# Attention and feed-forward layer on eight cores: score and value matmuls issued in groups of two key tiles

## The reference

```python
x = x + attn(layernorm(x), Wq, Wk, Wv, Wo)     # 16 heads of 64, rotary, softmax over 4096 keys
x = x + ffn(layernorm(x), w1, b1, w2, b2)      # two bitlinear layers, GELU between them
# bitlinear: activations rounded to 8 bits by row, weights to -1, 0, 1 times a scale
h = bitlinear(x, w1, b1)                       # 1024 -> 4096
h = gelu(h, approximate=False)
return bitlinear(h, w2, b2)                    # 4096 -> 1024
```

## Time and profile before

| | |
|---|---|
| median of the timed runs | 2846.5 us (2844.7 to 2848.4) |
| the profiled execution | 2838.8 us |
| its span on the slowest core, core 2 | 2837.2 us |
| spans of the 8 cores | 2820.6 to 2837.2 us |
| mean granted TensorE clock, core 2 | 0.853 |

### The profile page before, as it was taken

The page is one execution under the profiler, slowest core; times in us unless marked ns, Lnnn a source line. Parts: engine busy times, 40 slices in busy tenths (PEclk is TensorE's granted clock), DMA queues, the critical chain, the costliest instruction groups (busy, mean ns, idle before and its releaser), DMA issues.

```text
span 2837.2 us, 33149 instructions; the slowest of 8 cores (2820.6 to 2837.2 us)
## 1 busy us (share of the span) xinstructions
PE 2228.4 (79%) x8940; PEld 759.5 (27%) x8940; DVE 1067.8 (38%) x1941; ACT 1599.9 (56%) x2139; POOL 180.3 (6%) x345
## 2 busy tenths in 40 slices
PE   4679999888888888888888888563047988889888
PEld 1223333222222222222222222121013433334333
DVE  2434445311111111102222220287536666666564
ACT  3301112489988899988899889311413444434432
POOL 4211111000000000000000000111100000000000
PEclk8799999889988889888899889776557888888888
DMA  9633323301001010101111110475600000000000
GB/s 160 94 60 60 60 60 73 99 23 45 30 30 52 23 45 30 53 1 56 41 60 45 45 31 1 112 231 184 200 37 1 31 31 16 31 18 28 31 16 23
DMA packets 72194, 160.57 MB, mean 57 GB/s; under 512 B 8144, under 2 KB 41040, under 8 KB 70736
## 3 DMA queue, kind: packets, MB, share of 16 engines
q0 software_dynamic: 48544, 104.90, 16.2%
q1 hardware_dynamic: 23472, 53.55, 5.2%
HBM read 158.42 MB, written 29.36 MB: 66 GB/s over the span
## 4 chain that ended last, share of the span: by engine, by line
PE 42%; ACT 28%; DVE 12%; issue 10%; DMA 6%; DVEq 1%; ACTq 1%; POOL 0%; POOLq 0%; SPq 0%
ACT Et L686 24%; PE ps_b L1271 9%; PE ps_b L1318 8%; PE ps_k L405 6%; PE ps_v L380 4%; PE ps_tr L1302 3%; PE ps_cA L621 2%; PE ps_S L656 2%; DMA xb<-x_fm 2%; PE ps_cB L627 2%; DMA w2st<-w2T 2%; DVE wtmp L878 1%; DVE q1fm L1154 1%; PE ps_k L412 1%; PE ps_n L421 1%
## 5 line engine op out<-in xcount | busy, mean ns | idle before, releaser
L686 ACT ACTIVATE Et<-ps_S,negG 128x1024 bf16<-128x1024 f32 x1024 | 1046.7, 1174 | 85.8 <-PE ps_S L661 78.9
L656 PE MATMUL ps_S<-Qp,Kp 64*128 64x512 bf16 x1024 | 411.8, 407 | 120.4 <-ACT Et L686 72.3
L621 PE MATMUL ps_cA<-Et,V_sb 128*65 128x512 bf16 x1024 | 436.0, 426 | 43.6 <-DVEq L768 37.0
L661 PE MATMUL ps_S<-Qp,Kp 64*128 64x512 bf16 x1024 | 423.1, 418 | 0.0
L627 PE MATMUL ps_cB<-Et,V_sb 128*65 128x512 bf16 x1024 | 413.8, 404 | 0.0
L756 DVE COPY rlbc<-ps_rl 64x512 f32<-64x512 f32 x32 | 21.8, 683 | 766.3 <-PE ps_rl L638 766.3
L1271 PE MATMUL ps_b<-w1q,q1fm 128*128 128x512 bf16 x1024 | 255.3, 415 | 1.2 <-DVEq L1156 1.0
L656 PEld LDWEIGHTS ps_S<-Qp,Kp 64*128 64x128 bf16 x1024 | 93.6, 94 | 595.0 <-issue 595.0
L493 ACT ACTIVATE ksq<-krot 128x512 bf16<-128x512 bf16 x96 | 60.4, 629 | 297.1 <-DVEq L461 297.1
L1318 PE MATMUL ps_b<-w2q,q2fm 128*128 128x512 bf16 x1024 | 226.2, 382 | 2.0 <-DVEq L1186 2.0
L621 PEld LDWEIGHTS ps_cA<-Et,V_sb 128*65 128x65 bf16 x1024 | 113.3, 111 | 302.0 <-issue 295.4
(11 more groups left out here) (193 smaller groups left out, 2155.3 us busy)
## 6 DMA issues: line engine op xcount, KB each, us to landing
w1st_<-w1T POOLq DMA_DIRECT2D x64, 512.0 KB, 4.2
w2st<-w2T POOLq DMA_DIRECT2D x64, 512.0 KB, 4.7
xb<-x_fm POOLq DMA_DIRECT2D x64, 128.0 KB, 9.8
xr<-x_fm POOLq DMA_DIRECT2D x64, 128.0 KB, 5.5
kscr<-krot SPq DMA_DIRECT2D x64, 128.0 KB, 1.9
Kp<-kscr SPq DMA_DIRECT2D x8, 1024.0 KB, 4.9
xq<-x_tmq SPq DMA_DIRECT2D x16, 512.0 KB, 6.7
y1scr<-y1r SPq DMA_DIRECT2D x16, 512.0 KB, 5.9
```

Source lines behind the costliest of these rows:

```text
L621: e.matmul(ps2_cA[:], V_sb[:, jj * VBLK + (2 * m) * VW: jj * VBLK + (2 * m) * VW + VW], Et[itp % 4][:, 0:512], start=(jj == 0), stop=(jj = ...
L656: e.matmul(ps2_S[it % 2][:, 0:512], Kp[m % 2][0:64, j * 128:(j + 1) * 128], Qp[m % 2][0:64, qh * 512:(qh + 1) * 512], start=True, stop=Tru ...
L661: e.matmul(ps2_S[it % 2][:, 512:1024], Kp[m % 2][64:128, j * 128:(j + 1) * 128], Qp[m % 2][64:128, qh * 512:(qh + 1) * 512], start=True, s ...
L686: e.activation(Et[it % 4][:], ps2_S[it % 2][:], AF.Exp, bias=negG[:, m:m + 1], scale=1.0).then_inc(SM["aEX"], 1)
```

## The change

It has two parts. In the attention stage TensorE's loop goes over pairs of key tiles. For jp = 0, 2, ... 30 it issues AV(jp-4), AV(jp-3), S(jp), S(jp+1), so the order is S0, S1, rl_a; S2, S3, rl_b; AV0, AV1, S4, S5; AV2, AV3, S6, S7; and so on; after S31 come AV28 to AV31. The buffers, the waits in front of each instruction and the other engines' programs stay as they are. In the last stage the bias rows are spread through the two tiles of `ps4_b1` in place of `ps4_b2`, and the wait for the last round moves from the second product of tile 0 to its first.

```diff
-                    for j in range(NTT):
-                        it = it_of(m, qh, j)
-                        ...
-                        e.matmul(ps2_S[it % 2][:, 0:512], ...)
-                        e.matmul(ps2_S[it % 2][:, 512:1024], ...).then_inc(SM["pSC"], 1)
-                        if j >= 3:
-                            do_av(j - 3)
-                        if blk >= 1 and j == 1:
+                    for jp in range(0, NTT, 2):
+                        for jj in (jp - 4, jp - 3):
+                            if jj >= 0:
+                                do_av(jj)
+                        for j in (jp, jp + 1):
+                            it = it_of(m, qh, j)
+                            ...
+                            if it >= 2:
+                                e.wait_ge(SM["aEX"], it)
+                            e.matmul(ps2_S[it % 2][:, 0:512], ...)
+                            e.matmul(ps2_S[it % 2][:, 512:1024], ...).then_inc(SM["pSC"], 1)
+                        if blk >= 1 and jp == 0:
                             rl_mm_a(blk - 1)
-                        if blk >= 1 and j == 2:
+                        if blk >= 1 and jp == 2:
                             rl_mm_b(blk - 1)
-                    for jj in (NTT - 3, NTT - 2, NTT - 1):
+                    for jj in (NTT - 4, NTT - 3, NTT - 2, NTT - 1):
                         e.wait_ge(SM["aEX"], it_of(m, qh, jj) + 2)
                         do_av(jj)
...
-                e.matmul(ps4_b2[:, 0:512], ones_f1[:], outb[0][0:1, 0:512],
+                e.matmul(ps4_b1[0][:], ones_f1[:], outb[0][0:1, 0:512],
                          start=True, stop=True, skip_group_check=True)
-                e.matmul(ps4_b2[:, 512:1024], ones_f1[:],
-                         outb[0][0:1, 512:1024],
+                e.matmul(ps4_b1[1][:], ones_f1[:], outb[0][0:1, 512:1024],
...
-                e.tensor_copy(bdst[:, off:off + 512], ps4_b2[:, 0:512])
-                e.tensor_copy(bdst[:, off + 512:off + 1024],
-                              ps4_b2[:, 512:1024])
+                e.tensor_copy(bdst[:, off:off + 512], ps4_b1[0][:])
+                e.tensor_copy(bdst[:, off + 512:off + 1024], ps4_b1[1][:])
...
             def part_a1_mm(t):
                 e.wait_ge(SM["vTE"], 8 * (t + 1))
+                if t == 0:
+                    e.wait_ge(SM["vC2"], 5)
                 bl1_range(t, range(0, 4))
...
                 if t == 0:
                     e.wait_ge(SM["vW2q"], 32)
-                    e.wait_ge(SM["vC2"], 5)
```

More of the change, by code:

```diff
@@ new lines, in _ @@
+                    for jp in range(0, NTT, 2):
[4 more added lines that the diff above has]
+                            it = it_of(m, qh, j)
+                            if qh == 0 and j == 0:
+                                e.wait_ge(SM["dKQa" if m % 2 == 0
+                                             else "dKQb"],
+                                          32 * (m // 2 + 1))
+                            if it >= 2:
+                                e.wait_ge(SM["aEX"], it)
+                            e.matmul(ps2_S[it % 2][:, 0:512],
+                                     Kp[m % 2][0:64, j * 128:(j + 1) * 128],
+                                     Qp[m % 2][0:64,
+                                               qh * 512:(qh + 1) * 512],
+                                     start=True, stop=True,
+                                     tile_position=(0, 0),
+                                     skip_group_check=True)
+                            e.matmul(ps2_S[it % 2][:, 512:1024],
+                                     Kp[m % 2][64:128,
+                                               j * 128:(j + 1) * 128],
+                                     Qp[m % 2][64:128,
+                                               qh * 512:(qh + 1) * 512],
+                                     start=True, stop=True,
+                                     tile_position=(64, 0),
+                                     skip_group_check=True
+                                     ).then_inc(SM["pSC"], 1)
+                        if blk >= 1 and jp == 0:
```

## The result

The changed kernel takes 2908.8 us in the median of its runs against 2847.1 us of the kernel before beside it: ratio 1.0224, with a 95% interval of 1.0200 to 1.0247. It is slower by about 62 us; the interval's lower end lies just on two per cent. The forecast was 2920 us. Some executions of each kernel take a few per cent longer, with a lower granted clock on the cores of one die or both: ratios in this text compare the others alone, the medians take in all runs, and the profiles of pairs_rlb_behind_s2 and pairs_rlb_early were taken in such executions.

What follows compares the result with a forecast made beforehand. The exp on ScalarE was taken to set the steady pace, TensorE's chain through VectorE the block starts. Block start 51 us plus steady part 23 us gave 74 us on the 2846.5 us median: 2920 us, range 2868 to 2948.

Steps and rivals of the forecast that it cites:

- The start of a block: First exps of each block, E being exp 0's start: later rl_b and AV1 ahead of S4 delay exp 4 by 1.89 us.
- What comes back: Waits after exp 4 in each block: they shrink from 0.85 us by 0.25 us, leaving 1.64 us loss per block.
- The steady part: Exps 8 to 30: even S queued behind four AV matmuls comes 0.12 us late, 0.06 us per two exps, 23 us.
- some 384 short waits: Sign in the attention stage: ScalarE's line 686 waits some 75 us longer, in about 31 long and some 384 short ones.
- Block end and last stage: AV28 to AV31 after S31, and the bias broadcast with its moved wait: both were to cost nothing.
- The switches: TensorE's changes between half-array and full-array matmuls: about 0.10 us each, number halved, hidden where the exp sets the pace.
- TensorE sets the pace: Rival, steady part: saving 0.2 us for each of 512 pairs of iterations, 102 us, 2744 us; chance 0.04.
- Only the block start costs: Rival: even S in time, or more later waits come back; +18 to +57 us, centre 2892 us; chance 0.28.
- The change moves nothing: Rival, block start: VectorE or the clock absorbs the shifted rl_b; 0 to +18 us, about 2855 us; chance 0.03.
- The low clock lasts: Rival: longer TensorE idle pieces keep 1.2 GHz for one more pair of iterations per block, 25 us more, 2945; chance 0.07.

Runs made afterwards that it cites:

- pairs_rlb_behind_s2: The changed kernel with rl_b put back behind S2, in front of S3; 2877 us, 1.008 of the kernel before.
- pairs_rlb_early: The changed kernel with rl_b directly behind rl_a, in front of S2; 2826 us, 0.995 of the kernel before.
- pairs_early_busy: The changed kernel with rl_b in front of S2, S0 computed 4 times and S1 9 times; 2776 us, 0.974 of the kernel before.
- pairs_short_cb: The changed kernel with the cB matmul of every odd key tile covering 256 of its 512 queries; 2879 us in one run.
- last_stage_alone: The kernel before with only the change's second part, bias rows through other PSUM tiles and the wait moved; 2850 us, ratio 0.999.
- rlb_early_busy: The kernel before with rl_b directly behind rl_a, S0 computed 4 times and S1 9 times; 2757 us, ratio 0.970.
- rlb_early: The kernel before with rl_b moved from behind S2 to directly behind rl_a, in front of S2; 2802 us, ratio 0.981.

## Why the prediction was right

**The start of a block.** Forecast: rl_b 1.01 us later, AV1 ahead of S4, exp 4 at E + 7.73. Measured: E + 7.78, wait 3.64 us against 1.69. In 31 blocks this is 31 x 1.95 = 60 us (forecast 31 x 1.89 = 59). Undoing rl_b's part alone gave 35.7 us back, so both halves of this step were tested: rl_b by removal, AV1 by what remains (2.55 us against 1.69).

**What comes back.** Forecast 0.25 us a block. Of the 127.3 us, 31 x 3.64 = 113 are exp 4's and 1.3 are the first block's; 13 remain, against 27 before: 14 us, 0.45 us a block. The term was too small by 0.2 us a block, 6 us. The forecast had the clock rise ahead of S6 in about half of the blocks, to make exp 6 wait 0.81 us in one half and 0 to 0.3 us in the other. Instead S6's record is short (0.39 us, full clock) in all 31 blocks, the AV matmuls ahead of it have mostly run at the low clock, and exp 6 waits 0.28 to 0.50 us in 29 of them:

```profile
652.43 0.44 PE L627 MATMUL ps_cB<-Et,V_sb 128*65 128x512 bf16 x1
...
652.81 0.39 PE L661 MATMUL ps_S<-Qp,Kp 64*128 64x512 bf16 x1
```

The rise itself came about where it was put: the first short record lies 4.5 us behind AV0 in the mean (3.6 to 4.6), and 4.8 us before (3.0 to 6.5). One reading of the earlier trace rows was wrong without touching the sum: behind exp 4's wait there is one more where the last run has 27 exps, and three where it has 25, not two and four.

**The steady part.** Forecast 0.06 us in two exps, 23 us. Measured 0.048 us (1.029 against 1.005), over 25 distances in 31 blocks 18 us; pairs_early_busy gives 17 us and pairs_short_cb 18 us. The mechanism was right, the size a little too large: exp(j+1) was to start 3.14 us behind exp(j-2) for odd j, and starts 3.10 to 3.12 us behind it in nearly all cases, so that it is late by 0.095 us against 3.015 and not by 0.12. The lateness does not come evenly either: a late even exp is followed by one in time, and even exps follow each other after 2.01 and 2.11 us in turn. The odd S show the same, 2.00, 2.11 and 2.01 us apart at 614.88, 616.88, 618.99 and 621.00. The some 384 short waits that were to show it are absent, hidden in the overlap of the records. The 1.005 us of the forecast is right, as a distance between ends: it is the stretch less its first record of 1.11 us; the last record is 1.22 us long.

**The sum.** ScalarE's account for line 695 against 686: idle 127.3 - 78.9 = +48.4 us, busy 1058.8 - 1046.7 = +12.1 us, other idle time 8.0 - 6.6 = +1.4: +61.9 us, the stage's 61.7. The forecast was 51 + 23 = 74. That busy time rose by 12 and not by 18 comes from the overlap: 98 breaks became 62, and 36 x 0.1 = 4 us went the other way, which the forecast did not have; about 2 us more are the 4.24 us that the four first exps took in 23 blocks before, and 4.14 us now. The main terms missed by 2, 6, 5 and 6 us, all but the first to the same side, so the forecast's nearness does not come from errors that cancel.

**Edits costed at nothing.** Block end and last stage: nothing, as forecast (last_stage_alone 0.999).

**The switches.** Forecast 0.10 us each, and hidden. In the changed kernel S to cA takes 0.32 us (612.68 to 613.00), cB to S 0.32 (613.67 to 613.99), and AV matmuls follow each other after 0.21 to 0.24. That the change of tiles costs it, and not the score matmuls as such, is seen where rlb_early_busy repeats S without a change. Its pairs start 0.22 us apart:

```profile
838.38 0.38 PE L657 MATMUL ps_S<-Qp,Kp 64*128 64x512 bf16 x1
...
838.60 0.38 PE L657 MATMUL ps_S<-Qp,Kp 64*128 64x512 bf16 x1
```

The Trainium skill has each change of the tiling mode drain TensorE (TensorEngine Tiling (Array Packing), Key Properties). The trace agrees that a change costs something; a wait for the recorded end of the matmul (0.38 us) it does not show.

**The rivals.** "TensorE sets the pace" fell: TensorE had less to do (74% instead of 79%) and waited more for exps (235.9 us instead of 72.3), and the kernel was slower. "Only the block start costs" fell with pairs_short_cb and pairs_early_busy. "The change moves nothing" fell with the 61.7 us. "The low clock lasts" fell too: the longer idle pieces did not bring the clock down in the steady part (1.00 from 613 to 639 us), and core 2's mean granted clock is 0.850 against 0.853 before.

## What to carry to other kernels

An instruction's price is the price of what stands behind it in its queue: one small matmul a block (0.63 us in the trace), moved behind a score matmul that waits, cost 36 us in 31 blocks through VectorE, and moved ahead in the order of before it gained 45. Before grouping work to save switches, add up the way from the last wait in the queue to the instruction that the pacing engine needs, and compare it with that engine's own period; a fully busy share does not show that it is in time. Where an engine's clock falls in a pause, look at what the first instructions after the pause cost, and whether harmless repeats in the pause are cheaper.

## What the runs showed of the hardware

- A wait of ScalarE costs its idle time plus about 0.1 us: exps of 128x1024 that follow without a break end 1.005 us apart, and behind a break the record is 1.11 us long. 76 breaks fewer (rlb_early_busy against rlb_early) brought 7 us beyond the idle time itself. While the scores are always ready the records stretch, up to 1.31 us, without the pace changing. An exp that comes up to 0.1 us late shows no idle time at all, as the 1.029 us from exp to exp in the changed kernel do.
- A change between half-array score matmuls and full-array matmuls costs about 0.10 us each way at the full clock (0.31 to 0.34 us between starts, against 0.22 from AV to AV and also from S to S), and it is hidden here, where ScalarE sets the pace.
- The granted clock can be held by repeated matmuls: 11 pairs in each pause raised core 2's mean from 0.859 (rlb_early) to 0.892 and made the attention stage 37.8 us shorter (ratios 0.981 and 0.970). If the extra matmuls cost anything, it is small: ScalarE's waits for scores are 5.8 us in all.
